# When tiles of x are rounded, and which queue loads the first two batches' outputs

## What is computed

```
base = x @ W.T + b ;  lora = (x @ A[i]) @ B[i] * 2          # one adapter i per sequence
q, k, v = (base + lora) @ (w_q, w_k, w_v)                   # 32 heads of 32, 8 key/value heads
x = x + softmax(q k^T / sqrt(32)) v @ w_o
h = x @ weight[j].T                                         # one matrix j per sequence
gates = softmax of the 2 largest of 4 router logits of h
x = x + 4 * sum_e gates_e * (h @ A_e^T) @ B_e^T
```

## Time and profile before

| | |
|---|---|
| median of 3 runs | 1053.18 us (1052.08 to 1053.78) |
| the profiled execution | 1050.59 us, of which the span from first to last instruction is 1048.9 us |
| TensorE busy | 1013.4 us (97%), weight loads 820.2 us |
| VectorE, ScalarE, GpSimd busy | 633.5, 449.5, 234.0 us |
| mean granted TensorE clock | 0.988 of 2.4 GHz |
| transfers | 117.41 MB, 112 GB/s in the mean |

### The profile page before, as it was taken

The page is one execution under the profiler, slowest core; times in us unless marked ns, Lnnn a source line. Parts: engine busy times, 40 slices in busy tenths (PEclk is TensorE's granted clock), DMA queues, the critical chain, the costliest instruction groups (busy, mean ns, idle before and its releaser), DMA issues.

```text
span 1048.9 us, 17421 instructions
## 1 busy us (share of the span) xinstructions
PE 1013.4 (97%) x6934; PEld 820.2 (78%) x6934; DVE 633.5 (60%) x1071; ACT 449.5 (43%) x782; POOL 234.0 (22%) x224
## 2 busy tenths in 40 slices
PE   7999999999999999999999999999899999999997
PEld 6878787877678776787767787676589998988986
DVE  6562724667856578664776657654665655655653
ACT  5121223355754557554665556635422332323321
POOL 1000001123323233223332246643111111111100
PEclk9999999999999999999999999999999999999998
DMA  7030312111421124211232134453966756766531
GB/s 263 0 101 1 131 47 73 27 38 43 123 55 38 29 56 122 60 40 27 53 113 60 42 93 142 123 154 142 257 215 197 229 193 199 228 196 205 201 122 40
DMA packets 49888, 117.41 MB, mean 112 GB/s; under 512 B 7298, under 2 KB 26114, under 8 KB 45712
## 3 DMA queue, kind: packets, MB, share of 16 engines
q1 hardware_dynamic: 40080, 81.70, 26.4%
q0 software_dynamic: 9728, 34.61, 10.4%
HBM read 86.38 MB, written 18.89 MB: 100 GB/s over the span
## 4 chain that ended last, share of the span: by engine, by line
PE 90%; DMA 3%; DVE 3%; ACT 1%; SPq 1%; issue 1%; POOL 0%; ACTq 0%
PE psP L759 20%; PE psW L1043 17%; PE psF L254 11%; PE psG L1071 8%; PE psO L825 6%; PE psT L812 5%; PE psS L801 5%; PE psP L774 4%; PE psX L1286 3%; PE psO L829 2%; PE psY L1305 2%; PE psF L265 1%; DMA x_raw<-in_xT 1%; PE psM L836 1%; PE psP L740 1%; PE psP L742 1%
## 5 line engine op out<-in xcount | busy, mean ns | idle before, releaser
L673 DVE TENSOR_REDUCE nmax<-psS 128x2 f32<-128x512 f32 x256 | 164.5, 684 | 153.8 <-PE psS L801 152.1
L550 POOL TENSOR_TENSOR p_sum<-probs 128x512 f32<-128x512 f32 x128 | 167.6, 1310 | 372.6 <-ACT probs L600 372.3
L759 PE MATMUL psP<-x_hl,wq 128*128 128x512 f32 x960 | 235.1, 392 | 0.6 <-DVE q_stack L653 0.6
L759 PEld LDWEIGHTS psP<-x_hl,wq 128*128 128x128 f32 x960 | 175.2, 189 | 32.8 <-issue 0.8
L1043 PE MATMUL psW<-wq 128*128 128x256 f32 x1536 | 196.7, 283 | 1.6 <-DVE q_stack L653 1.2
L1043 PEld LDWEIGHTS psW<-wq 128*128 128x128 f32 x1536 | 190.3, 191 | 6.2 <-issue 1.3
L600 ACT ACTIVATE probs<-psT 128x512 f32<-128x512 f32 x256 | 139.2, 596 | 54.4 <-PE psT L812 53.9
L1052 ACT ACTIVATE cond_hi<-cond_raw 128x1024 fp32r<-128x1024 f32 x64 | 66.8, 1057 | 152.5 <-PE psG L1071 148.1
L1056 DVE TENSOR_TENSOR cond_lo<-cond_raw,cond_hi 128x1024 fp32r<-128x1024 f32 x64 | 78.3, 1235 | 89.1 <-ACT cond_hi L1052 89.0
L812 PE MATMUL psT<-q_stack,k_stack 98*128 98x512 f32 x256 | 90.1, 427 | 7.7 <-ACT probs L600 5.4
L653 DVE TENSOR_TENSOR q_stack<-psP,q_stack 32x512 fp32r<-32x512 f32 x128 | 87.8, 686 | 9.2 <-ACT q_stack L566 7.1
(11 more groups left out here) (122 smaller groups left out, 1252.8 us busy)
## 6 DMA issues: line engine op xcount, KB each, us to landing
cond_raw<-in_cond POOLq DMA_DIRECT2D x64, 512.0 KB, 4.1
x_raw<-in_xT SPq DMA_DIRECT2D x32, 256.0 KB, 3.9
q_stack<-q_stack SPq DMA_DIRECT2D x32, 256.0 KB, 3.1
o_scratch<-o_sb SPq DMA_DIRECT2D x64, 128.0 KB
o_raw<-rden_scratch SPq DMA_DIRECT2D x32, 256.0 KB, 5.4
o_raw<-o_scratch SPq DMA_DIRECT2D x8, 1024.0 KB, 8.8
x_sb<-in_xT SPq DMA_DIRECT2D x8, 1024.0 KB, 6.8
outT<-x_sb SPq DMA_DIRECT2D x32, 256.0 KB, 2.5
```

The lines of the kernel that those rows point to most:

```text
L550: pool.tensor_tensor(p_sum[:, heads], probs[:, 0, heads], probs[:, 1, heads], ALU.add).then_inc(sum_done, 1)
L673: dve.tensor_reduce(nmax[:, n % 2, 2 * hp:2 * hp + 2, qt], psS[:, i % 2].rearrange("p (h k) -> p h k", h=2), AX.X, ALU.max, negate=True).t ...
L759: mm = pe.matmul(out, wq[:, i, w, k * P:(k + 1) * P], x[:, k, part], start=(k == 0 and n_ == 0), stop=False)
```

## The change

Two things are changed. The tiles of x are split over the steps in another way: ScalarE rounds three of the next pair's tiles in step 11 and five in step 12 (before: six and two), and VectorE subtracts for three in step 12 and five in step 13 (before: six and two). And `load_o(0)` and `load_o(1)` are issued by GpSimd, in its hooks 9 and 14, and no longer by SyncE; the loads of cond's first four tiles move to hook 14 behind `load_o(1)`. The two batches get semaphores of their own.

```diff
@@ scalar, step(n)
-                for k in {11: range(0, 6), 12: range(6, KT)}.get(s, ()):
+                for k in {11: range(0, 3), 12: range(3, KT)}.get(s, ()):
                     split_x_hi(act, p + 1, k)
@@ vector, step(n)
-                for k in {12: range(0, 6), 13: range(6, KT)}.get(s, ()):
+                for k in {12: range(0, 3), 13: range(3, KT)}.get(s, ()):
                     split_x_lo(dve, p + 1, k)
@@ finish_stage
+    o_first = [sem(f"o_first_{c}") for c in range(2)]
+    def o_signal(n):
+        return o_first[n] if n < 2 else o_landed[n % 2]
     def load_o(sp, n):
...
-                         ).then_inc(o_landed[n % 2], 16)
-        sp.dma_start(o_land(n % 2), oT[n]).then_inc(o_landed[n % 2], 16)
+                         ).then_inc(o_signal(n), 16)
+        sp.dma_start(o_land(n % 2), oT[n]).then_inc(o_signal(n), 16)
@@ ahead_sync
-        if s == 8:
-            sp.wait_ge(before.proj_done, unit(PAIRS - 1, "q5") + 1)
-            for i in range(2):
-                sp.wait_ge(before.o_stored[i], 32 * G)
-            load_o(sp, 0)
...
             load_x(sp, 1)
-            load_o(sp, 1)
@@ normalise
-        dve.wait_ge(o_landed[c], 16 * (HG + 1) * (n // 2 + 1))
+        dve.wait_ge(o_signal(n), 16 * (HG + 1) * max(n // 2, 1))
@@ ahead_gpsimd
-        if s == 13:
+        if s == 9:
+            pool.wait_ge(before.proj_done, unit(PAIRS - 1, "q5") + 1)
+            for i in range(2):
+                pool.wait_ge(before.o_stored[i], 32 * G)
+            load_o(pool, 0)
+        if s == 14:
             pool.wait_ge(before.proj_done, PAIRS * NS)
+            load_o(pool, 1)
             load_cond(pool, 0, range(RAW))
```

## The result

The changed kernel takes **1072.49 us** in the median of 4 runs (1069.35 to 1074.51); the kernel before, run beside it, takes 1052.63 us (1050.61 to 1053.78, 4 runs). The ratio is 1.0188, with a 95% interval from 1.0156 to 1.0220: slower by 1.9%. The forecast was 1068, the range 1059 to 1074: the time lies inside, in its upper part. The 19.9 us more lie above the +11.5 to +17.5 to which the prediction gave 0.62; their interval, about 16.4 to 23.2, reaches into that. Its profiled execution took 1071.18 us, with a span of 1069.5 us (before: 1050.59 and 1048.9) and a mean granted clock of 0.983 (before: 0.988).

The account below looks back on a forecast made before the run. TensorE was taken to bound the kernel. Rounding +5.2, first load +7.5 and cond +1.8 gave +14.5 us on the profiled 1050.6, so 1065.1; the runs' median lies 2.6 higher: 1067.7, said as 1068, range 1059 to 1074.

Parts of the forecast that it names:

- What bounds the kernel: TensorE, busy 1013.4 of 1048.9 us, so the end moves only when it loses or regains idle time or clock.
- The rounding: Steps 12 and 13 of pairs 0 to 2: exponentials' wait gone, but TensorE waits for tile 3's low part; +5.2 us.
- the chain: Pair 2, maxima copied at 545.05, then q7, its low parts, two maxima and tile 3's subtraction on VectorE: ends 552.5.
- the half-clock term: TensorE running at 1.2 GHz after each longer wait at tile 3: 1.5 us a pair, 4.5 in all.
- The first load: Last pair: GpSimd issues the first batch's load 7.9 us later, so step 11's scores wait; +7.5 us with half clock.
- The half clock: Last pair, after ten idle microseconds before step 11's scores: half-clock stretch paid again, 0 to 1.6 us, taken as 1.5.
- How row maxima wait behind a load: Last pair, SyncE's queue: maxima issued behind the first load arrive only when it has landed; TensorE waits 2.32 us.
- the rival of the quick queue: GpSimd's five transfers land in 7.7 us or less, cond arrives in time: 1063.7 us; chance 0.20.
- Cond: After step 12, cond's first tiles land behind the second batch's load, delaying TensorE's first row of cond; +1.8 us.
- The rounding in time: Rival: tile 3's low part is ready near 549, rounding gives -10.2 us, total 1052.3, no change; chance 0.06.
- The worse case: Rival: queue needs 11.4 us and waits chain on, +9.1, +4 and 5.8, total +19, so 1072 us; chance 0.12.

Follow-up runs that it names:

- loads_early: Kernel before with loads on GpSimd's queue, rounding unchanged, first load in hook 7 instead of 9: 1053.87 us against 1051.85, ratio 1.0009.
- late_sync: Kernel before with the first load still on SyncE's queue but issued in step 10 behind the row maxima: 1058.93 us against 1053.37, single run.
- loads_alone: Changed kernel with the rounding of before, so only the loads' queue and cond behind it differ: 1063.82 us, ratio 1.0103.
- round_alone: Kernel before with only the changed kernel's rounding, three tiles and five, loads as before: 1058.89 us against 1052.44, ratio 1.0064.
- round_four: Kernel before with rounding and subtractions split four tiles and four, loads as before: 1047.56 us, ratio 0.9939.
- tile3_later: Kernel before with the changed rounding alone, and u split 3 and 5 instead of 4 and 4: 1051.06 us against 1052.44, ratio 0.9983.
- hook 8: Kernel before with loads on GpSimd's queue, rounding unchanged, first load in hook 8 instead of 9: 1057.51 us against 1051.85, single run.

## Why the prediction was right, step by step

- **What bounds the kernel.** Right: TensorE is busy 1017.2 us of 1069.5. Of the 20.6 us more, only 3.8 are in its busy time; the rest is idle time, nearly all at the places named ahead. All three terms came out above their forecast, and the sum fell into the range because the range reached far enough up.
- **The rounding, forecast +5.2 (0.7 to 5.8), measured +6.4.** The mechanism held, and the chain was worked out well: from the copy of the maxima to the first subtraction it takes 557.48 - 550.51 = 6.97 us, forecast 6.84. In pair 2 the outputs start 559.04 - 550.78 = 8.3 us after the scores, forecast 7.7. Half of the difference of 0.6 is that chain, the other half the matmuls of tile 3 (558.21 to 559.04, 0.83 us, forecast 0.5), which run partly at half clock (granted 0.58 from 558 to 561). Behind the outputs the pair loses another 1.50 - (8.26 - 7.86) = 1.1 us, which answers to the half-clock term (1.5, less the 0.2 that was lost there in before). So each pair came out some 0.4 us above its forecast (2.0, 2.1 and 1.1 of the 5.2), and the sum a little above the upper end. The half-clock term came true for all three pairs, here and with the rounding alone, where TensorE waits 3.7 us each time. As a rule for shorter waits it does not hold: in loads_early, whose rounding is that of before, the three waits at L812 are 1.1, 1.6 and 2.3 us, and only the second was followed by a granted clock below 1.00 (0.63 from 414 to 417; 1.00 from 277 to 283 and from 546 to 555). Single pairs of profiles with the same rounding differ by up to 1.4 us (pair 0 of late_sync against before).
- **The first load, forecast +7.5 (3.8 to 9.1), measured +10.35.** This is the term that was mis-sized, and both its parts lay too low. GpSimd issues the load where forecast: 674.46 - 6.94 = 667.52, forecast 667.56. The landing took 11.0 us where I chose SyncE's 9.9 and had 11.4 as the upper bound; with it the scores come 7.2 us late (688.53 - 674.38 - 6.94), forecast 6.0. The half clock cost 17.29 - 14.15 = 3.1 us, where I had 1.5 and an upper bound of 1.6. That bound was read from waits of 2 to 3 us and carried to a wait of 11 us, for which before had no row: after the long wait the stretch was 6.5 us of work and not 3 (in loads_alone some 4, behind the same wait).
- **How row maxima wait behind a load.** The prediction reads the earlier trace rows as one queue that delivers in the order of issue. That is more than the rows show: TensorE has the maxima at 669.23, and the load's last piece, issued at 661.40, landed 8.1 us later, at 669.5. What the runs show is that the wait stands wherever the load is issued ahead of these maxima on SyncE's queue (2.3 us in before, 2.9 in round_alone, 2.7 in round_four) and is gone where it is not (the changed kernel, loads_alone, late_sync).
- **The Trainium skill's figure.** Its page "DMA: Bandwidth & Descriptors", section "Anatomy of one DMA — SWDGE (gpsimd) path", would have this load in 6.8 us, as an estimate; the run shows 11.0, with the pieces landing 3.7 to 5.8 us after their own issues and the last 9.0. The measurement decides: the rival of the quick queue is wrong.
- **Cond, forecast +1.8 (0 to 4), measured +3.3.** For the first row it was exact: the first tile arrives 740.78 - 729.61 = 11.2 us after the second load's first issue (forecast 723.5 - 712.4 = 11.1), and the row is late by 18.95 - 17.29 = 1.7 us. But I let the loss end with that row. The second tile arrives 743.21 - 740.78 = 2.4 us after the first, forecast 1.25, and its row starts 745.77 - 726.05 = 19.7 us later than in before, which adds 0.8. The other 0.9 us arise further on and were not traced to a place.
- **The rivals.** The rounding in time: wrong, by the three waits. The worse case: right in its two ingredients (queue 11.0, its 11.4; cond +3.3, its +4) and near in the time, 1072, for it took those parts together; the clock's 1.6 us more is in none of the cases.
- **What the edits give.** The 5.4 us of waits for exponentials and the 2.3 us for the row maxima were real gains to be had: four tiles instead of three get 4.7 us, and an early, divided load 3.9. In the change both were spent on a later wait for the same data. Left open is what decides whether, and for how long, the clock falls behind a wait: behind the waits for cond it makes some 2 to 3 us between the profiles of tile3_later, hook 7 and hook 8 and the others.

## What to carry to other kernels

When work is moved from before a wait to behind it, look up the first reader of the last thing moved, and add up what stands before it in order on the engine that makes it: here one tile of eight decided between a loss of 6 us and a gain of 5. A load that is moved to a quieter queue takes the place in time of the engine that issues it; count the issue, its landing and the reader's place, and move it earlier by what the new order takes away. After that ask what the early transfer now runs beside: only when four of its five pieces went out a step earlier, and a copy that TensorE waits for landed after 5.5 us instead of 8.3, did the gain come.

## What the runs showed of the hardware that was not expected

- TensorE's clock after a long wait. After 11.2 us idle, the granted clock was 0.50 before the work began (684 to 688) and for 6.5 us of it, a loss of 3.1 us; behind the same wait in loads_alone it was low for some 4 us of work. In the kernel before, the work behind shorter waits ran at half clock for some 3 us; in loads_early two of three such waits (1.1 and 2.3 us) were followed by full clock.
- Two queues are not independent. While 2 MB came over GpSimd's queue, a 256 KB copy on SyncE's queue landed 8.2 us after its issue, against 3.2 in the kernel before, and released TensorE's scores 2.85 us late. With the broadcasts moved ahead of it, it landed after 5.5 us, in time.
- The same 2 MB took 11.0 to 11.1 us from GpSimd's first issue to the reader in hook 9, 9.5 in hook 8 and 12.4 to its landing in hook 7; from SyncE's queue it took 9.4 and 9.9.
- GpSimd spends 0.5 us of its own order on each issue (2.5 us for five). Issued a step earlier, they held up a sum that TensorE waited 1.14 us for, and beside GpSimd's run that followed a VectorE subtraction of 0.17 us lasted 5.48 us, for which TensorE waited 1.69 us more.
